# Graph attention on one core: the sort's digits in slots that ScalarE fills, one operation for the one-hots, a product and a sum for the picks

## The chip, the core and the metric

The kernel runs on one core of one Trainium2 chip. A core has TensorE (PE; its weight loads are PEld), VectorE (DVE), ScalarE (ACT), GpSimd (POOL) and SyncE (SP, which here only issues DMAs), each with its own instruction stream; they meet through semaphores. The metric is the device time of one execution in microseconds (us), the median of several.

## The reference

One layer of graph attention over 12500 nodes and 412500 edges, with a residual and a layer norm:

```python
qkv = x @ qkv_w + qkv_b                      # q, k: 4 heads x 8; v: 4 heads x 16
qe = q[s] * scale + (edge_attr @ q_rpe_w + q_rpe_b)
ke = k[t] + (edge_attr @ k_rpe_w + k_rpe_b)
ve = v[t] + (edge_attr @ v_rpe_w + v_rpe_b)
compat = einsum('ehd,ehd->eh', qe, ke)
attn = softmax of compat over the edges of each s
out = layernorm(x + segment_sum(ve * attn, s))
```

Here s is the node that gathers an edge's message and t the other end. The edges come sorted by t, but the softmax and the sum go by s.

## The kernel before

It has three stages. The tables stage counts the edges of each node s and computes keys, values and queries of all nodes. The sort stage writes, for every edge, a record of 100 floats to the place in DRAM that a counting sort by s gives it. The attend stage reads each node's records, in 98 blocks of 128 nodes, and computes softmax, sum and norm.

The change is in the sort. Its edges go in 808 units of 512 edges, each of four tiles of 128 (CT = 4). A node's number is split in two digits, the low 7 bits (128 values) and the rest (98 values); the arrays lo_f, hi_f and src_f hold both digits and the number for all edges. For a unit u:

- SyncE (load_loop, lines 526 to 539) loads attributes, numbers broadcast to all partitions (ids_b) and a window of the key and value table, into one of 8 slots. Before it reuses a slot it waits for the ranks and the features of unit u - 8. Each unit is a row of register steps, one table load and three DMA issues.
- VectorE makes one-hots of both digits (hots, lines 581 and 583); counts for each edge the earlier edges of its unit with the same number (ranks, line 592, four operations, each with a read of its accumulator); picks each edge's place from the table that TensorE looked up (picks, line 601, four custom operations, each with an accumulator read too); adds rank and place, and multiplies query and key (place, lines 612 and 613); sums the product over a head (total, line 617).
- TensorE adds the unit's counts to the table of free places (line 680, waits for hots and for the table copy), looks up the rows of the table (line 689) and computes the features (line 706).
- ScalarE makes the transposed one-hots (lines 724 to 733), copies the table from PSUM (line 742, waits for the counts of line 680; TensorE's next unit waits for it) and copies the records (line 717).
- GpSimd scatters the records, four indirect DMAs a unit (line 556), once place and total of the unit are done.

Each engine's order is written out by hand: 16 units at the head, then a loop whose body holds 8 units. VectorE's step u is: picks of u - 2, total of u - 3, ranks of u + 2, place of u - 2, one-hots of u + 2. ScalarE's step u: offsets of u + 2, table copy of u, turned of u + 2, records of u - 1.

## Time and profile before

| | us |
|---|---|
| median of 3 runs | 6195.86 (6191.55 to 6196.50) |
| the profiled execution | 6252.36 |
| its span, first to last instruction | 6250.6 |

The granted TensorE clock was 0.723 of full speed over the span. The profile comes from one execution, so durations and waits are read from it and set against its own 6252.36. A page of the profile gives each engine's busy time, and its groups of instructions with busy time, mean duration, and the engine's idle time just before them with what ended it ("issue": nothing that the profile shows; "remote": a semaphore whose last update it can't name). A timeline gives single instructions with their start and duration. The durations of consecutive instructions on one engine overlap a little, so what one costs its engine is read from start to start.

### The profile page before, as it was taken

Reading aid. Unit: us, or ns where it says so; the run is one execution under the profiler, and the core shown is the slowest. Engines: PE = TensorE matmul, PEld = TensorE weight load, DVE = VectorE, ACT = ScalarE, POOL = GpSimd, SP = SyncE. Lnnn points to the kernel's source line nnn. Section 1 sums busy time; section 2 is a strip of 40 time slices with the busy share of each in tenths; the row PEclk is TensorE's granted clock in tenths of the full one; section 3 lists DMA queues with packets and bytes.
Section 4 is the critical chain, followed back from the end, with each engine's and each line's share of the span. In section 5 each row is a group of like instructions: output and inputs, shape, how many; then the busy total and the mean of one; then the engine's idle time right before and its main releaser. Section 6 shows DMA issues by size and latency. Waiting matters only on the chain. (4 is left out here: it accounts for less than half of the span.)

```text
span 6250.6 us, 108230 instructions
## 1 busy us (share of the span) xinstructions
PE 3639.5 (58%) x22344; PEld 3313.1 (53%) x22344; DVE 4739.5 (76%) x18269; ACT 3094.1 (50%) x7584; POOL 3604.8 (58%) x4044
## 2 busy tenths in 40 slices
PE   5656555555555555555555655556555655486886
PEld 4545555555555455555555554545555555365665
DVE  9987777777777777777777777777777777698998
ACT  6965555555455555555555554545555545232332
POOL 0025666666666666666666666666666666564664
PEclk9986666666666766666666666676666666798999
DMA  3023333333333333333333333333333333697997
GB/s 81 19 63 113 111 108 111 108 109 107 112 110 108 111 108 111 108 111 109 108 111 108 111 111 106 111 108 111 108 111 108 111 108 112 233 363 278 365 363 264
DMA packets 423280, 848.16 MB, mean 136 GB/s; under 512 B 190271, under 2 KB 254072, under 8 KB 410362
## 3 DMA queue, kind: packets, MB, share of 16 engines
q1 hardware_dynamic: 305412, 399.40, 23.0%
q0 software_dynamic: 117824, 448.32, 19.5%
q14 instruction: 33, 0.27, 0.0%
q8 instruction: 11, 0.18, 0.0%
HBM read 671.35 MB, written 176.01 MB: 136 GB/s over the span
## 5 line engine op out<-in xcount | busy, mean ns | idle before, releaser
L556 POOL DMA_INDIRECT rec_dram<-recs,place_i x3232 | 3097.1, 958 | 1873.9 <-issue 1807.9
L592 DVE SCALAR_TENSOR_TENSOR matches<-ids_b,src_f,ps_const 128x128 bf16<-128x128 int16 (+3 forms) x3232 | 1646.0, 542 | 601.5 <-issue 559.7
L680 PE MATMUL ps_cnt<-hi_hot,lo_hot 128*128 128x98 bf16 x3232 | 383.2, 264 | 2113.3 <-DVE hi_hot L583 1071.6
L680 PEld LDWEIGHTS ps_cnt<-hi_hot,lo_hot 128*128 128x128 bf16 x3232 | 236.1, 123 | 2292.6 <-DVE hi_hot L583 1177.7
L689 PE MATMUL ps_look<-free_rec,lo_hotT 128*128 128x98 f32 x6464 | 1406.6, 388 | 1.2 <-ACT lo_hotT L730 1.2
L742 ACT ACTIVATE free_rec<-ps_cnt 128x98 f32<-128x98 f32 x808 | 198.8, 246 | 2412.7 <-remote 2244.6
L706 PE MATMUL ps_feat<-w_in,edge_in 115*128 115x128 f32 x6464 | 1325.8, 371 | 45.6 <-issue 44.0
L689 PEld LDWEIGHTS ps_look<-free_rec,lo_hotT 128*128 128x128 f32 x6464 | 1286.7, 295 | 1.5 <-ACT lo_hotT L730 1.5
L706 PEld LDWEIGHTS ps_feat<-w_in,edge_in 115*128 115x128 f32 x6464 | 1224.6, 281 | 52.4 <-issue 51.1
L1013 PE MATMUL ps_sum<-msg,ident 128*128 128x256 f32 x2744 | 624.3, 386 | 243.5 <-DVE msg L1227 243.5
L601 DVE CUSTOM_DVE_ANT_0 picked<-hi_hot,ps_look 128x98 f32<-128x98 bf16 x3232 | 643.7, 248 | 94.3 <-issue 90.0
L1013 PEld LDWEIGHTS ps_sum<-msg,ident 128*128 128x128 f32 x2744 | 518.9, 192 | 348.8 <-DVE msg L1227 281.4
L724 ACT ACTIVATE lo_hotT<-ids_b,minus_p 128x512 f32<-128x512 int16 x808 | 578.2, 716 | 5.7 <-DMA w_in<-kv_dram 5.7
L726 ACT ACTIVATE edge_in<-ids_b,minus_p 96x512 f32<-96x512 int16 x808 | 578.2, 716 | 0.0
L730 ACT ACTIVATE lo_hotT<-lo_hotT,one 128x512 f32<-128x512 f32 x808 | 576.9, 714 | 0.0
L733 ACT ACTIVATE edge_in<-edge_in,one 96x512 f32<-96x512 f32 x808 | 575.3, 712 | 0.0
L581 DVE TENSOR_TENSOR lo_hot<-lo_f,ps_const 128x512 bf16<-128x512 bf16 (+1 forms) x808 | 547.5, 678 | 19.9 <-issue 19.9
L592 DVE DVE_READ_ACCUMULATOR matches<-ids_b,src_f,ps_const 128x1 f32 x3232 | 261.4, 81 | 326.8 <-issue 309.7
L717 ACT ACTIVATE recs<-ps_feat 128x512 f32<-128x512 f32 x808 | 468.7, 580 | 22.7 <-remote 15.9
L583 DVE TENSOR_TENSOR hi_hot<-hi_f,ps_const 128x392 bf16<-128x392 bf16 (+1 forms) x808 | 446.1, 552 | 1.9 <-issue 1.6
L1172 ACT ACTIVATE ps_prob<-ps_lg,neg 128x56 f32<-128x56 f32 x392 | 109.2, 279 | 537.4 <-DVE neg L1062 537.4
L601 DVE DVE_READ_ACCUMULATOR2_ANT first<- 128x1 f32 x3232 | 256.1, 79 | 150.3 <-issue 147.3
(154 smaller groups left out, 3424.7 us busy)
## 6 DMA issues: line engine op xcount, KB each, us to landing
ids_b<-id_dram SPq DMA_DIRECT2D x808, 384.0 KB
rec_dram<-recs,place_i POOLq DMA_INDIRECT x3232
edge_in<-in_attr SPq DMA_DIRECT2D x808, 36.0 KB
w_in<-kv_dram SPq DMA_DIRECT2D x808, 36.0 KB
kv_dram<-y SPq DMA_DIRECT2D x14, 336.0 KB, 2.8
xt<-in_xT SPq DMA_DIRECT2D x14, 224.0 KB, 3.3
out_y<-y SPq DMA_DIRECT2D x6, 448.0 KB
src_i<-in_src_tiles SPq DMA_DIRECT2D x1, 1616.0 KB, 8.5
```

What stands on the lines that cost most here:

```text
L556: pool.indirect_dma_start(rec_dram[:, :], bass.IndirectOffsetOnAxis(place_i[j][:, m:m + 1], 0), recs[j][:, m, 0:REC], None).then_inc(scatt ...
L581: dve.tensor_tensor(lo_hot[j][:, :, :], lo_f[:, tiles].unsqueeze(2).broadcast_to((P, CT, P)), ps_const[:, 0:1, :].broadcast_to((P, CT, P)) ...
L592: last = dve.scalar_tensor_tensor(matches[j % NS][:, junk:junk + before], ids_b[j][:, 1, 0:before], src_f[:, bass.ds(u * CT + m, 1)], ps_c ...
L601: ins = dve.tensor_tensor_reduce(out=picked[j % NS][:, m, :], in0=hi_hot[j][:, m, :], in1=ps_look[j % NS][:, m, 0:NB], scale=1.0, scalar=0 ...
L680: last = nc.tensor.matmul(ps_cnt[:, 0:NB], lo_hot[j][:, m, :], hi_hot[j][:, m, :], start=False, stop=False, skip_group_check=True)
L689: last = nc.tensor.matmul(ps_look[j % NS][:, m, 0:NB], lo_hotT[j % NS][:, P * m:P * (m + 1)], free_rec[j % 2][:, :], start=True, stop=True)
L706: last = nc.tensor.matmul(ps_feat[j % 2][:, m, :], edge_in[j][0:K_ROWS, tile], w_in[j][0:K_ROWS, :], start=True, stop=True)
L724: act.activation(lo_hotT[j % NS][:, :], ids_b[j][:, 0, :], ACT.Abs, bias=minus_p[:, 0:1]).then_inc(lo_off, 1)
L726: act.activation(edge_in[j][0:WIN, :], ids_b[j][0:WIN, 2, :], ACT.Abs, bias=minus_p[0:WIN, 0:1]).then_inc(dst_off, 1)
L730: act.activation(lo_hotT[j % NS][:, :], lo_hotT[j % NS][:, :], ACT.Relu, scale=-1.0, bias=one[:, 0:1]).then_inc(lo_hotT_made, 1)
L733: act.activation(edge_in[j][0:WIN, :], edge_in[j][0:WIN, :], ACT.Relu, scale=-1.0, bias=one[0:WIN, 0:1]).then_inc(dst_hotT_made, 1)
L1013: last = nc.tensor.matmul(ps_sum[i][:, 0:SUM, :], ident[:, :], msg[i][:, k:k + SUM, :], start=(k == 0), stop=(k + SUM == S0))
```

## The change

The three arrays become one, dig_f, with the three numbers of an edge side by side. In the sort ScalarE copies the twelve numbers of a unit, five units ahead, into one of eight small slots (dig); VectorE reads them from there, at fixed addresses, as the scalars of the ranks and as the source of the one-hots. These are made by one operation for both digits (hot), with 128 columns for each digit. The four fused picks become one product over the unit (picks) and one sum (firsts). VectorE's step is put in another order: picks of u - 2, place of u - 3, one-hots of u + 2, ranks of u + 2, firsts of u - 2, total of u - 3. TensorE reads its one-hots from hot; its order, GpSimd's and SyncE's stay. The head is written out to match.

```diff
-        T["lo_f"] = digits.enter_context(nc.sbuf_tensor("lo_f", [P, NT], F32))
-        T["hi_f"] = digits.enter_context(nc.sbuf_tensor("hi_f", [P, NT], F32))
-        T["src_f"] = digits.enter_context(nc.sbuf_tensor("src_f", [P, NT], F32))
+        T["dig_f"] = digits.enter_context(nc.sbuf_tensor("dig_f", [P, NT, 3], F32))
...
-            dve.tensor_copy(src_f[:, :], src_i[:, :]).then_inc(narrowed, 1)
+            dve.tensor_copy(dig_f[:, :, 2], src_i[:, :]).then_inc(narrowed, 1)
...
-            act.activation(lo_f[:, :], lo_w[:, :], ACT.Copy).then_inc(widened, 1)
-            act.activation(hi_f[:, :], hi_w[:, :], ACT.Copy).then_inc(widened, 1)
+            act.activation(dig_f[:, :, 0], lo_w[:, :], ACT.Copy).then_inc(widened, 1)
+            act.activation(dig_f[:, :, 1], hi_w[:, :], ACT.Copy).then_inc(widened, 1)
...
-        lo_hot = [sb(f"lo_hot{c}", [P, CT, P], BF16) for c in range(NU)]
-        hi_hot = [sb(f"hi_hot{c}", [P, CT, NB], BF16) for c in range(NU)]
+        dig = [sb(f"dig{c}", [P, CT, 3]) for c in range(NU)]
+        hot = [sb(f"hot{c}", [P, CT, 2, P], BF16) for c in range(NU)]
...
             def hots(u, j):
-                tiles = bass.ds(u * CT, CT)
-                dve.tensor_tensor(lo_hot[j][:, :, :], lo_f[:, tiles].unsqueeze(2).broadcast_to((P, CT, P)),
-                                  ps_const[:, 0:1, :].broadcast_to((P, CT, P)), ALU.is_equal)
-                dve.tensor_tensor(hi_hot[j][:, :, :], hi_f[:, tiles].unsqueeze(2).broadcast_to((P, CT, NB)),
-                                  ps_const[:, 0:1, 0:NB].broadcast_to((P, CT, NB)), ALU.is_equal).then_inc(hots_made, 1)
+                dve.wait_ge(dig_made, u + 1)
+                dve.tensor_tensor(hot[j][:, :, :, :], dig[j][:, :, 0:2].unsqueeze(3).broadcast_to((P, CT, 2, P)),
+                                  ps_const[:, 0:1, :].unsqueeze(1).broadcast_to((P, CT, 2, P)), ALU.is_equal).then_inc(hots_made, 1)
...
-                        matches[j % NS][:, junk:junk + before], ids_b[j][:, 1, 0:before], src_f[:, bass.ds(u * CT + m, 1)],
+                        matches[j % NS][:, junk:junk + before], ids_b[j][:, 1, 0:before], dig[j][:, m, 2:3],
...
-            def pick(u, j, m):
-                if m == 0:
-                    dve.wait_ge(looked, u + 1)
-                ins = dve.tensor_tensor_reduce(
-                    out=picked[j % NS][:, m, :], in0=hi_hot[j][:, m, :], in1=ps_look[j % NS][:, m, 0:NB], scale=1.0, scalar=0.0,
-                    op0=ALU.mult, op1=ALU.add, accum_out=first[j][:, m:m + 1])
-                if m == CT - 1:
-                    ins.then_inc(placed, 1)
+            def picks(u, j):
+                dve.wait_ge(looked, u + 1)
+                dve.tensor_tensor(picked[j % NS][:, :, :], hot[j][:, :, 1, 0:NB], ps_look[j % NS][:, :, 0:NB], ALU.mult).then_inc(picked_all, 1)
+
+            def firsts(u, j):
+                dve.wait_ge(picked_all, u + 1)
+                dve.tensor_reduce(first[j][:, :], picked[j % NS][:, :, :], AX.X, ALU.add).then_inc(placed, 1)
...
                 if not ends(u, -2):
                     picks(u - 2, at(2))
-                total(u - 3, at(3))
+                place(u - 3, at(3))
                 if not ends(u, 2):
+                    prepare(u + 2, at(-2))
                     ranks(u + 2, *slot(j, turn, -2))
                 if not ends(u, -2):
-                    place(u - 2, at(2))
-                if not ends(u, 2):
-                    prepare(u + 2, at(-2))
+                    firsts(u - 2, at(2))
+                total(u - 3, at(3))
...
         def scalar_loop(act, general):
+            SOON = 5
...
+                if not ends(u, SOON):
+                    digits(u + SOON, slot(j, turn, -SOON)[0])
+
+            def digits(u, j):
+
+                if not starts(u, NU):
+                    act.wait_ge(ranked, u - NU + 1)
+                act.activation(dig[j][:, :, :], dig_f[:, bass.ds(u * CT, CT), :], ACT.Copy).then_inc(dig_made, 1)
+
+            for u in range(SOON):
+                digits(u, u)
```

How the order of instructions differs, in the loop's body. VectorE before, the end of a step's ranks and what follows up to the one-hots (the four picks and the total stand ahead of it; an ISA row between ranks sets an address; a rank's accumulator read is part of its row):

```order
L592 ISA
L592 SCALAR_TENSOR_TENSOR matches3,rank3<-ids_b3,src_f,ps_const 128x256
L592 ISA
L592 SCALAR_TENSOR_TENSOR matches3,rank3<-ids_b3,src_f,ps_const 128x384
L592 ISA
L592 SCALAR_TENSOR_TENSOR matches3,rank3<-ids_b3,src_f,ps_const 128x512
L612 TENSOR_TENSOR place_i7<-first7,rank7 128x4 [waits ranked,placed,kv_copied]
L613 TENSOR_TENSOR qk3<-recs7 128x128
L581 REGISTER_ALU
L581 TENSOR_TENSOR lo_hot3<-lo_f,ps_const 128x512
L583 REGISTER_ALU
L583 TENSOR_TENSOR hi_hot3<-hi_f,ps_const 128x392
```

And the picks before, at the start of VectorE's next step:

```order
L600 REGISTER_ALU
L601 ISA picked0,first0<-hi_hot0,ps_look0 128x98 [waits looked]
L601 ISA first0 128x1
L601 ISA picked0,first0<-hi_hot0,ps_look0 128x98
L601 ISA first0 128x1
L601 ISA picked0,first0<-hi_hot0,ps_look0 128x98
L601 ISA first0 128x1
L601 ISA picked0,first0<-hi_hot0,ps_look0 128x98
L601 ISA first0 128x1
```

VectorE now, one whole step (picked, place_i, hot, matches, first, recs are what picks, place, one-hots, ranks, firsts and total write):

```order
L598 TENSOR_TENSOR picked3<-hot7,ps_look3 128x392 [waits looked]
L609 TENSOR_TENSOR place_i6<-first6,rank6 128x4 [waits ranked,placed,kv_copied]
L610 TENSOR_TENSOR qk2<-recs6 128x128
L580 REGISTER_ALU
L581 TENSOR_TENSOR hot3<-dig3,ps_const 128x1024 [waits dig_made]
L590 SCALAR_TENSOR_TENSOR matches3,rank3<-ids_b3,dig3,ps_const 128x128 [waits loaded3,ranked]
L590 SCALAR_TENSOR_TENSOR matches3,rank3<-ids_b3,dig3,ps_const 128x256
L590 SCALAR_TENSOR_TENSOR matches3,rank3<-ids_b3,dig3,ps_const 128x384
L590 SCALAR_TENSOR_TENSOR matches3,rank3<-ids_b3,dig3,ps_const 128x512
L602 TENSOR_REDUCE first7<-picked3 128x4 [waits picked_all]
L614 TENSOR_REDUCE recs6<-qk2 128x4x4 [waits dotted]
```

The picks' eight rows became one here and one near the end, the address rows between the ranks are gone, and the one-hots stand ahead of the ranks. ScalarE before, one step (lo_hotT and edge_in are the transposed one-hots, free_rec the table copy, recs the records):

```order
L724 ACTIVATE lo_hotT0<-ids_b4,minus_p 128x512 [waits looked,loaded4]
L726 ACTIVATE edge_in4<-ids_b4,minus_p 96x512
L742 ACTIVATE free_rec1<-ps_cnt 128x98 [waits counted]
L729 REGISTER_ALU
L730 ACTIVATE lo_hotT0<-lo_hotT0,one 128x512 [waits lo_off]
L733 ACTIVATE edge_in4<-edge_in4,one 96x512 [waits dst_off]
L717 ACTIVATE recs1<-ps_feat1 128x4x128 [waits scattered1,feats]
```

ScalarE now, the same step:

```order
L725 ACTIVATE lo_hotT0<-ids_b4,minus_p 128x512 [waits looked,loaded4]
L727 ACTIVATE edge_in4<-ids_b4,minus_p 96x512
L743 ACTIVATE free_rec1<-ps_cnt 128x98 [waits counted]
L731 ACTIVATE lo_hotT0<-lo_hotT0,one 128x512 [waits lo_off]
L734 ACTIVATE edge_in4<-edge_in4,one 96x512 [waits dst_off]
L718 ACTIVATE recs1<-ps_feat1 128x4x128 [waits scattered1,feats]
L760 ISA [waits ranked]
L760 ACTIVATE dig7<-dig_f 128x12
```

Two rows are added at the end of the step, the copy of the digits and the setting of its address, and one register step (line 729) is gone; the operations ahead of them stand as before.

## Rows read from the trace of the kernel before

**Rows 1.** The page: busy time of the engines, then VectorE's costliest groups (section 5).

```profile
PE 3639.5 (58%) x22344; PEld 3313.1 (53%) x22344; DVE 4739.5 (76%) x18269; ACT 3094.1 (50%) x7584; POOL 3604.8 (58%) x4044
...
L592 DVE SCALAR_TENSOR_TENSOR matches<-ids_b,src_f,ps_const 128x128 bf16<-128x128 int16 (+3 forms) x3232 | 1646.0, 542 | 601.5 <-issue 559.7
L601 DVE CUSTOM_DVE_ANT_0 picked<-hi_hot,ps_look 128x98 f32<-128x98 bf16 x3232 | 643.7, 248 | 94.3 <-issue 90.0
```

**Rows 2.** Busy time in one stretch of 500 us inside the sort.

```profile
core 0: us, PE busy (x) PEld busy (x) DVE busy (x) ACT busy (x) POOL busy (x), PEclk, DMA share, GB/s
3000.00:3500.00 500.00, 281.74 (x1626) 262.70 (x1627) 359.89 (x1716) 256.11 (x491) 312.77 (x327) 0.67 0.36 110
```

**Rows 3.** Line 556, GpSimd's scatters: first and last start, idle time before them.

```profile
L556 POOL DMA_INDIRECT rec_dram<-recs,place_i x3232: 952/958/1216, 413.3 to 5376.6; - x191
...
  issue: 1807.9, 3154
```

**Rows 4.** Who waited for whom, 1000 to 5000 us (us in total, times, longest).

```profile
ACT free_rec L742 <- remote: 1845.4, 306, 12.1
DVE matches L592 <- issue: 715.8, 1184, 2.0
...
SPq L532 <- remote: 322.5, 161, 7.2
```

**Rows 5.** Timeline of VectorE: start us, us, engine line op out<-in.

```profile
3028.88 0.15 DVE L612 TENSOR_TENSOR place_i<-first,rank 128x4 int32<-128x4 f32 x1
...
3029.15 0.67 DVE L581 TENSOR_TENSOR lo_hot<-lo_f,ps_const 128x512 bf16<-128x512 bf16 x1
3029.75 0.54 DVE L583 TENSOR_TENSOR hi_hot<-hi_f,ps_const 128x392 bf16<-128x392 bf16 x1
3030.22 0.24 DVE L601 CUSTOM_DVE_ANT_0 picked<-hi_hot,ps_look 128x98 f32<-128x98 bf16 x1
...
3030.93 0.27 DVE L617 TENSOR_REDUCE recs<-qk 128x16 f32<-128x128 f32 x1
3031.13 0.33 DVE L592 SCALAR_TENSOR_TENSOR matches<-ids_b,src_f,ps_const 128x128 bf16<-128x128 int16 x1
...
3033.00 0.15 DVE L612 TENSOR_TENSOR place_i<-first,rank 128x4 int32<-128x4 f32 x1
```

**Rows 6.** The same, a few us later; in brackets the idle time before.

```profile
3038.16 0.35 DVE L592 SCALAR_TENSOR_TENSOR matches<-ids_b,src_f,ps_const 128x128 bf16<-128x128 int16 x1 [0.44 <-issue]
3038.88 0.08 DVE L592 DVE_READ_ACCUMULATOR matches<-ids_b,src_f,ps_const 128x1 f32 x1 [0.38 <-issue]
3040.96 0.48 DVE L592 SCALAR_TENSOR_TENSOR matches<-ids_b,src_f,ps_const 128x256 bf16<-128x256 int16 x1 [1.99 <-issue]
```

**Rows 7.** Timeline of GpSimd: a run of eight scatters and the next one.

```profile
3012.51 0.96 POOL L556 DMA_INDIRECT rec_dram<-recs,place_i  x1 [2.39 <-issue]
...
3021.34 0.96 POOL L556 DMA_INDIRECT rec_dram<-recs,place_i  x1 [0.30 <-issue]
3024.78 0.96 POOL L556 DMA_INDIRECT rec_dram<-recs,place_i  x1 [2.48 <-issue]
```

**Rows 8.** Timeline of SyncE's queue: two DMAs of three units.

```profile
3015.26 0.03 SPq L534 DMA_DIRECT2D edge_in<-in_attr  x1
...
3021.82 0.73 SPq L539 DMA_DIRECT2D w_in<-kv_dram  x1
3024.30 0.31 SPq L534 DMA_DIRECT2D edge_in<-in_attr  x1
...
3026.80 0.32 SPq L534 DMA_DIRECT2D edge_in<-in_attr  x1
```

**Rows 9.** Timeline of ScalarE in the same stretch.

```profile
3017.44 0.71 ACT L726 ACTIVATE edge_in<-ids_b,minus_p 96x512 f32<-96x512 int16 x1
3024.17 0.25 ACT L742 ACTIVATE free_rec<-ps_cnt 128x98 f32<-128x98 f32 x1 [6.02 <-remote]
```

**Rows 10.** Timeline of TensorE in the same stretch.

```profile
3018.30 0.51 PE L680 MATMUL ps_cnt<-hi_hot,lo_hot 128*128 128x98 bf16 x4 [0.29 <-DVE hi_hot L583]
```

More of the change, by code:

```diff
@@ L102, in tables_stage @@
     iota_row, iota_f, iota_p, ident, later = (T[k] for k in ("iota_row", "iota_f", "iota_p", "ident", "later"))
-    lo_f, hi_f, src_f, q_tab = (T[k] for k in ("lo_f", "hi_f", "src_f", "q_tab"))
+    dig_f, q_tab = T["dig_f"], T["q_tab"]
     base, deg, w_attr = (T[k] for k in ("base", "deg", "w_attr"))
@@ L399, in higher @@
                     last = act.activation(s_hi[i][:, k, :], ps_half[:, 0:NB + 1], ACT.Sign, scale=-1.0,
-                                          bias=hi_f[:, bass.ds(GT * g + GT - SIGNS + k, 1)])
+                                          bias=dig_f[:, bass.ds(GT * g + GT - SIGNS + k, 1), 1])
                 last.then_inc(hi_signs, 1)
@@ L437, in sort_stage @@
     iota_p, ident, later = (T[k] for k in ("iota_p", "ident", "later"))
-    lo_f, hi_f, src_f, base, w_attr, win_row, flag = (T[k] for k in ("lo_f", "hi_f", "src_f", "base", "w_attr", "win_row", "flag"))
+    dig_f, base, w_attr, win_row, flag = (T[k] for k in ("dig_f", "base", "w_attr", "win_row", "flag"))
     deg, y, more = (T[k] for k in ("deg", "y", "more"))
@@ L491, in sort_stage @@
         lo_off, dst_off = sem("lo_off"), sem("dst_off")
+        dig_made, picked_all = sem("dig_made"), sem("picked_all")
         kv_got = [sem(f"kv_got{c}") for c in range(NU)]
@@ L618, in total @@
                                   AX.X, ALU.add).then_inc(totalled, 1)
-            def picks(u, j):
-                for m in range(CT):
-                    pick(u, j, m)
             def prepare(u, j):
@@ L632, in step, with ahead @@
                     picks(u - 2, at(2))
-                total(u - 3, at(3))
+                place(u - 3, at(3))
                 if not ends(u, 2):
+                    prepare(u + 2, at(-2))
                     ranks(u + 2, *slot(j, turn, -2))
                 if not ends(u, -2):
-                    place(u - 2, at(2))
-                if not ends(u, 2):
-                    prepare(u + 2, at(-2))
+                    firsts(u - 2, at(2))
+                total(u - 3, at(3))
             def head():
+                at = lambda u: u % NU
+                def ahead(*units):
+                    for v in units:
+                        prepare(v, at(v))
+                        ranks(v, at(v), v // NU)
                 prepare(0, 0)
@@ L645, in head @@
                 prepare(1, 1)
-                at = lambda u: u % NU
                 for u in range(HEAD - 4):
                     picks(u, at(u))
+                    firsts(u, at(u))
                     place(u, at(u))
@@ L655, in head @@
                 ranks(u + 1, at(u + 1), (u + 1) // NU)
+                firsts(u, at(u))
+                ahead(u + 2)
                 place(u, at(u))
-                for v in (u + 2, u + 3):
-                    ranks(v, at(v), v // NU)
-                    prepare(v, at(v))
+                ahead(u + 3)
                 total(u, at(u))
                 picks(u + 1, at(u + 1))
-                for v in (u + 4, u + 5):
-                    ranks(v, at(v), v // NU)
-                    prepare(v, at(v))
-                place(u + 1, at(u + 1))
+                ahead(u + 4)
+                firsts(u + 1, at(u + 1))
+                ahead(u + 5)
             if general:
@@ L679, in step @@
                 for m in range(CT):
-                    last = nc.tensor.matmul(ps_cnt[:, 0:NB], lo_hot[j][:, m, :], hi_hot[j][:, m, :], start=False, stop=False,
+                    last = nc.tensor.matmul(ps_cnt[:, 0:NB], hot[j][:, m, 0, :], hot[j][:, m, 1, 0:NB], start=False, stop=False,
                                             skip_group_check=True)
```

## The prediction

> **What bounds the kernel now.** The page comes first: VectorE is the busiest engine at 76%, yet idle a quarter of the time, and its largest groups are line 592 (ranks) and line 601 (picks) [rows 1]. The stretch table says the same of the sort alone: 360 of 500 us for VectorE, 313 for GpSimd, 282 for TensorE, 256 for ScalarE [rows 2]. GpSimd's scatters run from 413.3 to 5376.6 us, 4963 us of the 6250.6; its 3232 scatters, four a unit, make 808 units of 6.14 us [rows 3]. All of the change that counts is in this stage.
>
> Next, what ends VectorE's idle time. Its largest group is "issue": 716 us in 1184 pieces before line 592, inside 4000 us, released by nothing that the profile shows [rows 4]. The timeline shows it in two ways. In one, a unit takes 3033.00 - 3028.88 = 4.12 us and no instruction waits [rows 5]. In the other, consecutive instructions without any wait between them start about 0.7 us apart, or a multiple of it (3038.16, 3038.88, 3040.96), while they run for 0.08 to 0.48 us [rows 6]. So 6.14 - 4.12 = 2.02 us a unit, 1630 us in all, is time in which VectorE has work and is not handed it.
>
> This is not VectorE's alone. GpSimd scatters two units in one run: first start 3012.51, last 3021.34, next run 3024.78 [rows 7]. Inside it SyncE, whose steps for a unit are all sequencer work, needs 3024.30 - 3015.26 = 9.04 us for a unit; just after it, 3026.80 - 3024.30 = 2.50 [rows 8]. ScalarE is held in the same stretch: TensorE has the counts of a unit at 3018.30 + 0.51 = 3018.81, and the copy that waits for them starts at 3024.17, when SyncE is quick again [rows 9, 10]. This late wake-up is most of ScalarE's 1845 us on "remote" [rows 4]. I call such stretches held, and the others free: a held stretch goes with a run of scatters, beginning and ending near 1.9 us after it (an estimate from the ends 3022.30 and 3024.17). A scatter takes 0.96 + 0.30 = 1.26 us [rows 7], a unit 5.05, so about 4.9 us of each 6.14 are held.
>
> **The change part by part.** VectorE's work without stalls, by start to start [rows 5]:
> - Removed: one-hots 0.60 + 0.47, picks 3030.93 - 3030.22 = 0.71; together 1.78.
> - Added, none of it in the trace. One-hots of 1024 columns: 120 more columns (512 against 392) cost 0.13 us, 1.08 ns each, so 0.60 + 512 x 1.08 ns = 1.15. The one operation makes 128 columns of the high digit where 98 were made, so fusing saves a start and pays 120 columns. The product of 392 columns from the same kinds of memory: 0.47, as line 583. The sum over 392: line 617 sums 128 in 3031.13 - 3030.93 = 0.20, plus 264 x 1.08 ns, 0.48. Together 2.10. Bounds for product and sum together: 0.71 (as the picks) and 1.2 (both as the 512-column operation). I take 0.95, since the column counts match.
> - Net: +0.32 us a unit, between +0.08 and +0.57. Were VectorE simply busy, 808 x 0.32 = 259 us slower.
>
> VectorE's instructions: before 21 on the engine a unit (8 for picks, 8 for ranks with their accumulator reads, 2 one-hots, 2 place, 1 total) and 6 address steps, of which four stand at the ranks; after 14 and one. 27 become 15, with a wait or two more (picked_all, dig_made). Stalls come by the instruction, 0.7 us each, and 2.02 us are about three a unit. Twelve fewer more than cover three, if what VectorE is handed is limited by number. I take its own stalls to go: it then needs 4.12 + 0.32 = 4.44 us a unit, and is 1.7 us early. The new own wait picked_all has place, one-hots and four ranks between producer and waiter (3 us of work), so it is met on arrival. dig_made is filled five units ahead. The one-hots now stand ahead of the ranks, so TensorE gets them earlier in a step by the ranks' 3033.00 - 3031.13 = 1.87 us [rows 5].
>
> ScalarE: one more copy of 12 columns (at most the 0.25 us of line 742 [rows 9]), one address step and a wait for ranks of three units back, long done. Busy 256.11/500 x 6.14 = 3.14 becomes 3.4 a unit: under 4.44, so nothing, unless it is on the path, then up to 0.25. ScalarE is late now because counts come after it asks for them; with one-hots early they come before. TensorE's program is the same, 3.5 us a unit [rows 2].
>
> Outside the loop: the three widenings write every third word; they are a few us in all and I add nothing.
>
> **What is late next.** Two things stand under 6.14.
> - GpSimd: 5.05 us of scatters plus its gap between runs, 2.48 [rows 7]. With runs of m units a unit takes 5.05 + 2.48/m: 6.29 at two, 5.88 at three, 5.67 at four. VectorE early means more finished units when GpSimd looks, so longer runs.
> - SyncE: its program is unchanged, and in a held stretch it needs 9.04 us for a unit. With 4.9 held us a unit it does 4.9/9.04 = 0.54 of its work there, and the other 0.46 costs 1.15 free us: 6.05 us a unit. Longer runs leave fewer free us, so loads fall behind, VectorE and ScalarE wait for them, GpSimd runs dry, and a free stretch comes. It waits for a free slot 322 us in 652 units, 0.5 a unit [rows 4], so the lower bound is 5.64; upper bound 6.05. Since the waits are themselves late wake-ups I stay near the upper: 5.98.
>
> Sum: 808 x (6.14 - 5.98) = 129 us off the profiled 6252.4 (span 6250.6 and 1.8 around it): 6123. The timed runs' median is 56.5 us under the profiled one, so 6067.
>
> A rule speaks against this. No row names what slows the sequencers. The Trainium skill ("Runtime: NRT & Kernel Launch", Instruction fetch mechanics) holds that instruction fetch is hidden, because dispatch is slower than the fills, save at a taken branch. By that rule fewer instructions relieve nothing and the sum would be +259 us. The trace disagrees in part: the 0.7 us steps of rows 6 lie far from a loop's branch.
>
> **The rivals.**
> - Much faster. SyncE's slack is real (5.64) and runs reach four units (5.67): 808 x 0.47 = 380 us off, 5816. For it: SyncE's waits; VectorE's large reserve. Against: its 9.04 us. 19%.
> - No change. GpSimd asks for a unit's total as soon as the previous one is queued, and in a held stretch hears of it only at its end; total stays last in the step, so runs stay at two units and 6.14 stands: 6196. 11%.
> - Slower, by VectorE. The stalls are a share of time and not of instructions (for it: they stop at once when the run ends), so 2.02 us stay and the longer operations are paid in full: 6196 + 259 = 6455; at half, 6325. It decides if less than 0.32 us a unit of stall goes. 18%.
> - Slower, by ScalarE: the extra copy delays the table copy that TensorE waits for, and its wait in a held stretch costs another late wake-up: 808 x 0.25 = 200 us, 6396. Against: ScalarE is idle half the time. 6%.
>
> **How the numbers follow.** Forecast 46%, by itself 5990 to 6150: 6067. The whole range reaches to the half-way points of the outer rivals and leaves about two in ten out: 5800 to 6290. A change under 0.2% (12 us) can't be told from none. Faster: 45 of the forecast's 46, the 19, and 3 of no change, 67%; the same: 9%; slower: 24%.
>
> **What would show it.** Idle on "issue" before VectorE's ranks falls from 716 us to under 200; its one-hots take near 1.2 us, product 0.55, sum 0.55; ScalarE's "remote" before the table copy shrinks; runs of scatters of three or more units appear; and new idle time stands at the waits for loads (VectorE's ranks or ScalarE's line 725, released by a DMA), with SyncE no longer waiting. The forecast is wrong if VectorE still stalls in 0.7 us steps, if runs stay at eight scatters, or if a unit falls below 5.8 us with SyncE still waiting.

## The result, and the profile after

| | before | after |
|---|---|---|
| median, us | 6196.18 (6191.55 to 6199.01, 4 runs) | 6412.99 (6404.22 to 6440.81, 4 runs) |
| profiled execution, its span | 6252.36, 6250.6 | 6414.70, 6413.0 |
| granted TensorE clock | 0.723 | 0.727 |

The ratio is 1.0355, 95% interval [1.0339, 1.0371]: 217 us slower, where 129 us faster was forecast, and above the forecast's range of 5800 to 6290. A later comparison gave 1.0366 [1.0349, 1.0384]. The profiled execution of the kernel before was itself 56 us above its median, so the two profiles show 162 of the 217 us.

The page of the kernel after, busy time and VectorE's groups of the change (against [rows 1]; busy us, mean ns of one, idle before it):

```profile
PE 3405.3 (53%) x22344; PEld 3084.7 (48%) x22344; DVE 4787.4 (75%) x12613; ACT 3172.6 (49%) x8392; POOL 3606.2 (56%) x4044
...
L590 DVE SCALAR_TENSOR_TENSOR matches<-ids_b,dig,ps_const 128x128 bf16<-128x128 int16 (+3 forms) x3232 | 1572.8, 541 | 3.6 <-issue 3.6
...
L598 DVE TENSOR_TENSOR picked<-hot,ps_look 128x392 f32<-128x392 bf16 x808 | 448.4, 555 | 1339.3 <-remote 1194.6
...
L581 DVE TENSOR_TENSOR hot<-dig,ps_const 128x1024 bf16<-128x1024 f32 x808 | 979.8, 1213 | 0.9 <-issue 0.9
...
L602 DVE TENSOR_REDUCE first<-picked 128x4 f32<-128x392 f32 x808 | 448.0, 554 | 11.6 <-issue 10.8
```

What was forecast of VectorE came: 12613 instructions for 18269; the idle time before the ranks fell from 601.5 us (559.7 of it on issue) to 3.6; one-hots take 1.21 us, product and sum 0.55 each. But 1339 us of idle time now stand before the product. GpSimd's scatters after (against [rows 3]: first and last start, idle time before them):

```profile
L556 POOL DMA_INDIRECT rec_dram<-recs,place_i x3232: 952/958/1216, 415.6 to 5539.1; - x191
...
  issue: 1488.6, 3143
  DVE place_i L609: 509.0, 73
```

They take 5123.5 us, 160 more than before, of 162 more in the span: 6.34 us a unit for 6.14. Nearly all of it is idle time of GpSimd, of which 509.0 us now stand in 73 waits, 7 us each, for VectorE's place. Who waited for whom, 1000 to 5000 us (against [rows 4]):

```profile
ACT free_rec L743 <- remote: 1766.4, 254, 17.9
...
PE ps_cnt L679 <- ACT free_rec L743: 1060.7, 179, 16.4
DVE picked L598 <- remote: 930.0, 163, 11.9
...
POOL rec_dram L556 <- DVE place_i L609: 370.9, 52, 9.1
PE ps_feat L705 <- issue: 356.5, 357, 2.6
```

From the starts of all scatters follows how long the runs are. A run ends here where GpSimd idles for more than 1.5 us, its gap is that idle time, and a cycle goes from its first scatter to the next run's first. Each cell has the number of cycles, their mean length, the mean gap, and the cycle's length for each unit (four scatters) in it, in us. Runs of other lengths, most of them cut inside a unit by a pause of 1.66 us, are left out (35 before, 28 after).

| scatters in the run | before: cycles, mean, gap, a unit | after |
|---|---|---|
| 4 | 42, 6.70, 1.95, 6.70 | 32, 8.98, 4.24, 8.98 |
| 8 | 306, 12.19, 2.38, 6.10 | 7, 14.48, 4.22, 7.24 |
| 12 | 30, 18.22, 2.71, 6.07 | 142, 17.89, 3.01, 5.96 |
| 16 | none | 57, 26.09, 5.34, 6.52 |
| 20 | none | 9, 34.23, 7.61, 6.85 |

Runs did get longer, as forecast, but their gaps grew with them, and single units came between. Runs of three units are no dearer than the runs of two were before (5.96 us a unit against 6.10); the loss stands in runs of four and five units and in single ones. Where the line at 1.5 us is put moves the counts (at 1.3 us, 172 runs of twelve and 35 of sixteen) and not this picture. The timeline after shows what happens inside a run, in four pieces: VectorE, ScalarE, TensorE, and GpSimd's run of twelve (start, us, instruction, idle before it).

```profile
3033.47 0.28 DVE L614 TENSOR_REDUCE recs<-qk 128x16 f32<-128x128 f32 x1
3041.96 0.56 DVE L598 TENSOR_TENSOR picked<-hot,ps_look 128x392 f32<-128x392 bf16 x1 [8.22 <-remote]
```

```profile
3033.20 0.71 ACT L727 ACTIVATE edge_in<-ids_b,minus_p 96x512 f32<-96x512 int16 x1
3042.11 0.25 ACT L743 ACTIVATE free_rec<-ps_cnt 128x98 f32<-128x98 f32 x1 [8.20 <-remote]
```

```profile
3027.58 1.10 PE L688 MATMUL ps_look<-free_rec,lo_hotT 128*128 128x98 f32 x8
...
3031.03 0.33 PE L679 MATMUL ps_cnt<-hot 128*128 128x98 bf16 x4 [1.33 <-issue]
...
3034.89 0.36 PE L705 MATMUL ps_feat<-w_in,edge_in 115*128 115x128 f32 x1 [1.17 <-issue]
3037.01 0.27 PE L705 MATMUL ps_feat<-w_in,edge_in 115*128 115x128 f32 x1 [1.77 <-issue]
3039.11 0.37 PE L705 MATMUL ps_feat<-w_in,edge_in 115*128 115x128 f32 x1 [1.83 <-issue]
3042.51 0.49 PE L679 MATMUL ps_cnt<-hot 128*128 128x98 bf16 x4 [3.03 <-ACT free_rec L743]
```

```profile
3024.88 0.96 POOL L556 DMA_INDIRECT rec_dram<-recs,place_i  x1 [2.72 <-issue]
...
3038.95 0.96 POOL L556 DMA_INDIRECT rec_dram<-recs,place_i  x1 [0.30 <-issue]
```

Counting products, lookups, copies and counts from the first unit on tells which belong together: the product at 3041.96 needs the lookup that ended at 3027.58 + 1.10 = 3028.68, and the copy at 3042.11 the counts that ended at 3031.03 + 0.33 = 3031.36. Both engines came to their wait at 3033.7 and 3033.9, long after its condition was met, and went on 2.0 and 2.2 us after the run's end at 3039.91. TensorE meanwhile started one matmul every 2.1 us without any wait, and SyncE made a step about every 0.7 us (from its table load at 3031.98 to the first DMA issue of its next unit at 3038.38 it needs 6.4 us; right after the run, from 3042.08 to 3042.74, 0.7). So this is not a late wake-up from an unmet wait: inside a long run VectorE and ScalarE stand still, TensorE and SyncE crawl, and GpSimd alone keeps its pace. The label "remote" stands for it. Counted so over units 60 to 739, all 186 pauses over 1.5 us before the product and all 278 before the table copy had their condition met before the engine arrived. In the kernel before that was so in 80 of ScalarE's 315; in the other 235 the condition was met while it stood, and it stood on for 5.5 us (median).

### The profile page after: what moved, and what is told of

It reads as the page before. It is cut to its first block and busy times, and to the rows that moved or that the text cites. A ratio compares the mean times of both kernels' runs of the same rounds, so it can differ in the third digit from the quotient of the medians.

```text
span 6413.0 us, 99854 instructions
## 1 busy us (share of the span) xinstructions
PE 3405.3 (53%) x22344; PEld 3084.7 (48%) x22344; DVE 4787.4 (75%) x12613; ACT 3172.6 (49%) x8392; POOL 3606.2 (56%) x4044
## 5 line engine op out<-in xcount | busy, mean ns | idle before, releaser
L590 DVE SCALAR_TENSOR_TENSOR matches<-ids_b,dig,ps_const 128x128 bf16<-128x128 int16 (+3 forms) x3232 | 1572.8, 541 | 3.6 <-issue 3.6
L598 DVE TENSOR_TENSOR picked<-hot,ps_look 128x392 f32<-128x392 bf16 x808 | 448.4, 555 | 1339.3 <-remote 1194.6
L679 PE MATMUL ps_cnt<-hot 128*128 128x98 bf16 x3232 | 351.9, 248 | 2064.3 <-ACT free_rec L743 1266.1
L679 PEld LDWEIGHTS ps_cnt<-hot 128*128 128x128 bf16 x3232 | 252.9, 119 | 2210.2 <-issue 2076.4
L688 PE MATMUL ps_look<-free_rec,lo_hotT 128*128 128x98 f32 x6464 | 1268.3, 360 | 3.6 <-DVE first L602 2.8
L688 PEld LDWEIGHTS ps_look<-free_rec,lo_hotT 128*128 128x128 f32 x6464 | 1154.0, 268 | 4.4 <-ACT lo_hotT L731 3.2
L581 DVE TENSOR_TENSOR hot<-dig,ps_const 128x1024 bf16<-128x1024 f32 x808 | 979.8, 1213 | 0.9 <-issue 0.9
L602 DVE TENSOR_REDUCE first<-picked 128x4 f32<-128x392 f32 x808 | 448.0, 554 | 11.6 <-issue 10.8
L398 ACT ACTIVATE s_hi<-ps_half,dig_f 128x99 bf16<-128x99 f32 x1212 | 303.6, 366 | 56.8 <-PE ps_sign L358 56.6
L1238 DVE TENSOR_TENSOR msg<-rec,ps_prob 128x1280 f32<-128x1280 f32 x196 | 287.9, 1469 | 2.0 <-ACT prob_s L1194 1.4
```

What stands on the lines that cost most here:

```text
L581: dve.tensor_tensor(hot[j][:, :, :, :], dig[j][:, :, 0:2].unsqueeze(3).broadcast_to((P, CT, 2, P)), ps_const[:, 0:1, :].unsqueeze(1).broad ...
L590: last = dve.scalar_tensor_tensor(matches[j % NS][:, junk:junk + before], ids_b[j][:, 1, 0:before], dig[j][:, m, 2:3], ps_const[:, CT - m: ...
L679: last = nc.tensor.matmul(ps_cnt[:, 0:NB], hot[j][:, m, 0, :], hot[j][:, m, 1, 0:NB], start=False, stop=False, skip_group_check=True)
L688: last = nc.tensor.matmul(ps_look[j % NS][:, m, 0:NB], lo_hotT[j % NS][:, P * m:P * (m + 1)], free_rec[j % 2][:, :], start=True, stop=True)
```

## The experiments

One thing first, since every number below depends on it. I call the executions that were timed together on one chip a session. The kernel before itself took (medians) either 5391 to 5400 us or 6196 to 6273 us in a session; all its executions in one session agreed within 0.3%, and one chip showed both levels in different sessions. I call these free and held sessions. In a free one SyncE's register steps follow each other at 0.16 us (mean from start to start; 0.35 in the held profile of the kernel before) through scatters 0.3 us apart, and GpSimd alone is the bound: 5.06 us a unit. Comparisons are within a session.

**Four edits of one kind each.** The first is the changed kernel with the order of before (`picks(u-2); total(u-3); ranks(u+2); firsts(u-2); place(u-2); prepare(u+2)`).

> The changed kernel's operations and slots, with the order of steps of the kernel before: picks of u - 2, total of u - 3, ranks of u + 2, firsts and place of u - 2, one-hots of u + 2. Theory A (VectorE, no longer stalled, arrives early at the wait for TensorE's lookups, is woken late in a held stretch, and GpSimd's scatters then gather in longer runs with longer gaps): the cause is that VectorE is ahead, whatever the order, so the time stays near the changed kernel's 6413, within 60 us. Theory B (the new order is the cause: place and total of a unit come a step later, behind the wait for the lookup): the time falls below 6200. Theory C (the longer operations are simply paid): 6413 within 20 us, and VectorE's idle time before picks stays.

The second is the kernel before, with `dig[j][:, :, 0:1]`, `dig[j][:, :, 1:2]` and `dig[j][:, m, 2:3]` for lo_f, hi_f and src_f, and ScalarE's copies.

> The kernel before with only the digit slots: ScalarE copies twelve numbers a unit, VectorE's ranks and its two one-hot operations read them from fixed addresses; the fused picks and the order stay. VectorE has 21 instructions a unit and one address step instead of six. Theory A (stalls go by the number of VectorE's instructions and steps; being ahead is what hurts): part of the 716 us of issue stalls before the ranks goes, VectorE waits for lookups in their place, and the time is between the two kernels, 6200 to 6350. Theory C (longer operations): no operation is longer, so it is not slower than 6196, and faster by up to 100 us. Theory D (ScalarE's copy): 6350 to 6413.

The third has the copies, and nobody reads them: `dig_f[:, tiles, 0:1]` for lo_f, and so on.

> The kernel before with ScalarE's copy of the digits alone: nobody reads the slots, VectorE reads the long array as before (every third word of it). Prices ScalarE's extra instruction, address step and wait. Theory D (ScalarE's copy is what costs: it delays the table copy): 6350 or more. Theories A, B and C: within 40 us of 6196.

The fourth is the changed kernel with VectorE's steps shifted:

```diff
-                    picks(u - 2, at(2))
-                place(u - 3, at(3))
+                    picks(u - 3, at(3))
+                place(u - 4, at(4))
...
-                    firsts(u - 2, at(2))
-                total(u - 3, at(3))
+                    firsts(u - 3, at(3))
+                total(u - 4, at(4))
```

> The changed kernel with picks and firsts of u - 3 and place and total of u - 4 in VectorE's step u, one unit later than now: TensorE has one more unit of time for the lookup that VectorE asks for. Theory A: VectorE's idle time before line 598 (1339 us in the changed kernel) falls by half or more; if that wait is what costs, the time falls to 6250 or below; if the late wake-ups then only move to ScalarE and TensorE, whose chain of count, table copy and next count is the same, it stays within 50 us of 6413. Theory C (longer operations): no change, 6413 within 30 us.

Measured, in a free session: 5403.5, 5401.7, 5403.3 and 5408.7 us beside 5399.6, ratios 1.0008, 1.0004, 1.0006 and 1.0017, intervals about ±0.001. The first two once more (5394.7 and 5393.6 beside 5391.3) and the first a third time (5396.9 beside 5394.1) were free too. They decide nothing of the 217 us; they show that without holding the parts of the change cost 0.2% at most, though VectorE works 4826.6 us in the first. The waits of its third run, 1000 to 4500 us:

```profile
ACT recs L716 <- DMA rec_dram<-recs,place_i: 1238.9, 525, 7.7
PE ps_feat L703 <- ACT recs L716: 1112.4, 502, 7.6
...
POOL rec_dram L556 <- issue: 810.8, 2660, 0.3
```

ScalarE and TensorE wait for scatters, and GpSimd never idles over 0.3 us. The line that headed [rows 4], ScalarE's wait before the table copy, does not appear.

**The changed kernel again.**

> The changed kernel itself, with the kernel before on the same chip. In the runs so far on this chip the kernel before takes 5400 us and not 6196: its traces show no held stretch and GpSimd's scatters follow each other at 0.3 us. If held stretches are what the change costs time by, it is within 10 us of the kernel before wherever these are missing, and about 217 us slower where the kernel before takes 6196. If the longer operations or the order cost by themselves, it is slower on both.

A held session: 6430.6 beside 6197.4, ratio 1.0366. The loss is real where sequencers are held. The changed kernel as it stands was never timed in a free one.

**Versions side by side in one execution.** Since nothing here chooses whether a session is held, I put several versions into one kernel: VectorE's loop over the units is cut into parts, each with its own step, as in `for k in range(3): part(dve, old_order(k + 1), PARTS[k], PARTS[k + 1])`. The pace of a part is (last start - first start)/(scatters - 1) x 4. Each of these kernels with parts was executed once, beside the kernel before.

> Four versions of the sort in one execution, one after the other, each over about 192 units, so that they are compared on one chip: (1) VectorE's operations and order of before, numbers from the long array, no copies by ScalarE (units 16 to 207), (2) the same with the digit slots filled by ScalarE and read by VectorE (208 to 399), (3) the changed kernel's operations in the old order (400 to 599), (4) the changed kernel's operations in its own order (600 to 791). The pace is read from GpSimd's scatters; in the kernel before it was between 6.08 and 6.14 us a unit in all of these stretches, in the changed one between 6.30 and 6.37. Theory A (being ahead, whatever the order): part 2 between 6.1 and 6.3, part 3 near 6.3, part 4 near 6.33. Theory B (the order): parts 1 to 3 at 6.14 or less, part 4 at 6.33. Theory C (longer operations simply paid): part 2 at 6.1, parts 3 and 4 at 6.33. Theory D (ScalarE's copies): parts 2 to 4 at 6.33. On a chip where the kernel before takes 5400 all parts run at GpSimd's 5.06.

A held session (6319.7, before 6197.0). Its scatters, a row for each part:

```profile
L564 POOL DMA_INDIRECT rec_dram<-recs,place_i x768: 952/958/1039, 522.1 to 1688.0; - x192
```
```profile
L564 POOL DMA_INDIRECT rec_dram<-recs,place_i x768: 952/958/1068, 1689.2 to 2849.9; - x192
```
```profile
L564 POOL DMA_INDIRECT rec_dram<-recs,place_i x800: 952/958/1042, 2856.2 to 4118.1; - x160
```
```profile
L564 POOL DMA_INDIRECT rec_dram<-recs,place_i x768: 952/958/1082, 4121.3 to 5342.4; - x192
```

6.08, 6.05, 6.32 and 6.37 us. Neither the order (0.05 between the last two) nor the slots and copies (-0.03) are the cause: it lies in the operations. How small a difference counts depends on the picks. In the kernel before, with fused picks, the pace over 80 units stays between 6.11 and 6.15; in the second profile of the changed kernel it goes from 6.24 to 6.52, and over 152 units, the length of the parts below, from 6.32 to 6.44 (6.27 to 6.43 in the first). So with product and sum differences under some 0.2 aren't told from none, with fused picks those under 0.05.

**Which operation, and whether its work or its number counts.** Part 3 adds `dve.tensor_tensor(spare[:, 0:2, :], ...)` over 256 columns, part 4 four operations of 4 columns, all between ranks and place, read by nobody.

> Again several versions in one execution, in the old order of steps and all with the digit slots, to tell which operation costs the 0.31 us a unit that lay between the second and the third part of the run before (6.02 and 6.33). (1) slots alone, units 32 to 183; (2) with the one operation for both one-hots, 184 to 335 (one instruction less, its work 0.08 us longer); (3) slots and one more VectorE operation of 256 columns, some 0.3 us, whose result nobody reads, 336 to 487; (4) slots and four more VectorE operations of 4 columns each instead, 488 to 639; (5) slots with picks as product and sum, 640 to 799 (six instructions less with the accumulator reads, 0.24 us longer). Theory C (VectorE's work is simply paid, microsecond by microsecond): (1) 6.02, (2) 6.1, (3) 6.33, (4) 6.2 to 6.4, (5) 6.27. Theory A (fewer instructions let VectorE run ahead into unmet waits, and longer runs of scatters come of it): (2) 6.02 to 6.1, (3) at most 6.1, (4) at most 6.1, since both slow VectorE down and hide nothing, (5) 6.25 or more. Theory E (instructions are what is rationed in held stretches): (4) is clearly above (3). Where the kernel before takes 5400 all parts run at 5.06.

A held session (6303.0, before 6249.3). First the part with slots alone, then those with four small operations, and with product and sum:

```profile
L565 POOL DMA_INDIRECT rec_dram<-recs,place_i x608: 956/962/1038, 620.1 to 1549.3; - x152
```
```profile
L565 POOL DMA_INDIRECT rec_dram<-recs,place_i x609: 956/962/1246, 3414.2 to 4369.2; - x153
```
```profile
L565 POOL DMA_INDIRECT rec_dram<-recs,place_i x637: 955/962/1069, 4369.2 to 5375.8; - x160
```

Runs are counted with the same 1.5 us, away from a part's edges:

| part | us a unit | runs of 8, of 12 or more |
|---|---|---|
| slots, fused picks | 6.12 | 44, 16 |
| and one operation for the one-hots | 6.13 | 44, 15 |
| and one more operation of 256 columns | 6.15 | 52, 8 |
| and four more of 4 columns | 6.28 | 71, 1 |
| product and sum for the picks | 6.33 | 0, 46 |

The one large operation takes 0.42 us, and the next instruction starts 0.33 us after it; it costs 0.02 us a unit, which isn't told from none. The four small ones keep the engine for 0.30 us, up to the start of the next, and cost 0.16. So beside fused picks VectorE's microseconds are not paid one by one (theory C falls), while four more instructions are paid for (theory E holds, on this one pair). The picks as product and sum cost 0.21 although they are six instructions fewer, and with them runs of two units are gone. Longer runs alone don't explain that yet: with fused picks and no small operations added, the runs of twelve took 6.05 to 6.12 us a unit in the parts of these two kernels, as the runs of eight did (6.03 to 6.11); beside product and sum, in the same old order, runs of twelve took 6.18 and 6.19.

**Around product and sum.** Part 2 puts `firsts(u - 2)` directly behind `picks(u - 2)`; parts 3 and 4 add work as above; part 5 does picks, sum and place of u - 3.

> Versions with picks as product and sum, in one execution, all with the digit slots, two one-hot operations and the old order; the part with these picks took 6.33 us a unit in the run before, the one with the fused picks 6.12. (1) as there, units 32 to 183; (2) the sum directly behind the product, as the fused picks do it, 184 to 335; (3) the sum late again, and four more operations of 4 columns each, which make the number of VectorE's instructions nearly that of the fused picks, 336 to 487; (4) instead one more operation of 256 columns, 0.3 us, 488 to 639; (5) picks, sum and place one unit later, 640 to 799. Theory A (with few instructions VectorE runs ahead into waits that are not yet met and wakes late from them): (1) 6.33, (2) 6.3, (3) 6.2 or less, (4) 6.25, (5) 6.2 or less. Theory E (every VectorE instruction is rationed in held stretches, and the late sum costs by itself): (2) 6.15, (3) 6.45, (4) 6.35, (5) 6.33. Where the kernel before takes 5400 all parts run at 5.06.

A held session (6489.6, before 6258.2): 6.34, 6.47, 6.48, 6.50 and 6.40 us. Product and sum cost as much in the first part of a kernel as in the last, so their place in it is not the cause. Theory A said that more instructions or a later lookup would heal it. Nothing did: that form of it, waits unmet on arrival, is wrong, as the timeline above shows too. The added work of parts 3 and 4 (0.14 and 0.17) isn't told from none here: part 2, without any, is 0.13 above part 1. One thing in part 3 does speak for run length. Its four small operations brought runs of two units back, some 30 of them beside 25 of three, and in this one part the runs of two took 6.18 us a unit and those of three 6.71.

**Runs kept short.** GpSimd waits, before some units, until the scatters of the unit before have landed:

```diff
                 if not starts(u, LAG):
+                    sent, sent_turn = slot(j, turn, LAG + 1)
+                    if most and (j - LAG) % most == 0:
+                        pool.wait_ge(scattered[sent], 16 * CT * sent_turn + 16 * CT)
```

> GpSimd is made to stop between scatters: before every second unit (or every unit, or every fourth) it waits until the scatters of the unit before have landed, so that a run can't be longer than that. All with the digit slots, two one-hot operations, the old order. (1) fused picks, no stop, units 32 to 139; (2) fused picks, stop every second unit, 144 to 283; (3) fused, every unit, 288 to 331; (4) picks as product and sum, every unit, 336 to 379; (5) the same, every second unit, 384 to 523; (6) every fourth unit, 528 to 651; (7) no stop, 656 to 799. Theory A in the form that is left (what costs is that runs of scatters get longer: three and four units instead of two, with gaps longer than in proportion): (1) 6.1, (2) 6.1 to 6.2, (5) 6.2 or less and so faster than (7) at 6.33, (6) like (7). If product and sum cost whatever the runs are: (5) is not below (7), and 0.2 or more above (2). Parts (3) and (4): about 5.05 us of scatters and a gap of 2.4 or more a unit, 7.4 or more, both alike. Where the kernel before takes 5400: (1) and (7) 5.06, the stops 1 to 2.4 us for each.

> The same kernel with stops once more, since the run before fell where the kernel before takes 5394 us and no sequencer is held; there the stops cost 2.1 us each. Parts: (1) fused picks, no stop, units 32 to 139; (2) fused, stop every second unit, 144 to 283; (3) fused, every unit, 288 to 331; (4) product and sum, every unit, 336 to 379; (5) every second unit, 384 to 523; (6) every fourth, 528 to 651; (7) no stop, 656 to 799. Where sequencers are held: if long runs of scatters are what product and sum cost by, (5) is 6.2 or less against 6.33 or more in (7), and (2) about (1) at 6.1. If product and sum cost whatever the runs are, (5) is 0.2 or more above (2), and not below (7).

The first fell in a free session (6048.4, before 5394.2): 5.06 without stops, 6.12 with a stop every second unit for either kind of picks, 7.62 and 7.61 with one every unit. The second was held (6462.7, before 6272.5). Its rows of product and sum, stopped every second unit, every fourth, and not at all:

```profile
L565 POOL DMA_INDIRECT rec_dram<-recs,place_i x560: 956/962/1081, 2937.6 to 3785.8; - x187
```
```profile
L565 POOL DMA_INDIRECT rec_dram<-recs,place_i x497: 955/962/1072, 3812.3 to 4599.7; - x166
```
```profile
L565 POOL DMA_INDIRECT rec_dram<-recs,place_i x572: 955/962/1074, 4623.7 to 5535.1; - x191
```

6.07, 6.35 and 6.38 us a unit; fused picks took 6.14 without stops and 6.10 with one every second unit, and both kinds 7.67 and 7.68 with one every unit. With runs of two units product and sum cost nothing, and an added wait makes the sort 0.3 us a unit faster. The stop every fourth unit (6.35) isn't told from no stop.

**The whole changed kernel with stops**, before units 0, 3 and 6 of each eight, or before every second.

> The changed kernel whole, with GpSimd waiting before units 0, 3 and 6 of each eight until the scatters of the unit before have landed, so that runs are of three, three and two units. Where sequencers are held: in the changed kernel the cycles of three units took 17.89 us, 5.96 a unit, and what made it 6.33 were the longer and the single ones. If long runs are the cost, this gives 5.9 to 6.0 a unit, 6020 to 6110 in all, faster than both kernels. If three units are already too long (gaps of 3.7 instead of 2.8 as with the old order): 6250 to 6400. Where they are not held (the kernel before at 5395): 3 stops of 2.1 us in eight units, 0.8 us a unit, about 6040.

> The changed kernel whole, stopped in the same way before every second unit. Where sequencers are held: 6.07 a unit as in the part with product and sum, about 6200, 210 us under the changed kernel and level with the kernel before; if the changed kernel's own order or one-hots cost beside the runs, 6300 or more. Where they are not held: 4 stops of 2.1 us in eight units, 1.05 us a unit, about 6240.

A held session, before 6251.4. Up to three units a run: 6498.8, ratio 1.0394 [1.0377, 1.0412]. Two: 6222.9, ratio 0.9956 [0.9939, 0.9973]. So the stops take the whole loss of the change away where sequencers are held, and leave it 0.4% under the kernel before. This kernel was not timed in a free session, where the same stops in the parts cost 1.06 us a unit. Its scatters, and its waits from 1000 to 5000 us:

```profile
L556 POOL DMA_INDIRECT rec_dram<-recs,place_i x3232: 956/962/1217, 415.2 to 5347.4; - x191
```
```profile
PEld ps_feat L708 <- issue: 1652.6, 387, 6.7
ACT recs L721 <- DMA rec_dram<-recs,place_i: 1400.5, 387, 6.0
```

Its 363 cycles of two units take 12.07 us with a gap of 2.23. The waits before the table copy and before the product are no longer among the nine largest, and ScalarE's largest is the one for scatters, as in a free session. With stops for three a run, 150 cycles of three units take 18.66 us (gap 3.72), 122 of two 12.87 (gap 2.93) and 53 single ones 8.57. My expectation of 6020 to 6110 for it was wrong: cutting the runs of four units off saves nothing (1.0394 times the kernel before, against 1.0355 and 1.0366 without stops), and next to runs of three even those of two are dearer, 6.44 us a unit against 6.03.

**The picks alone undone** in the whole changed kernel (the four fused picks at the step's start, no late sum), and the slots alone.

> The changed kernel whole with one part of it undone: the picks are the four fused operations of the kernel before, at the step's start, and the late sum is gone. Slots, ScalarE's copies, the one operation for the one-hots and the new order stay. Where sequencers are held: if the product and sum are what lets runs grow to three units, runs are of two units again, 6.0 to 6.1 a unit, and the time is that of the kernel before or up to 1% less; if the new order or the early one-hots do it too, runs of three stay and the time is 2% or more above it. Where they are not held: that of the kernel before within 0.2%.

> The kernel before whole with the digit slots alone, once more, for a chip where sequencers are held: in the run by parts this took 6.02 us a unit against 6.07 with the long array beside it. 808 x 0.05 = 40 us less than the kernel before, 0.65%, if that difference is real; within 0.2% if it was only the chance of where the parts lay. Where they are not held: 5394 to 5402 as before.

A free session: 5399.3 and 5394.2 beside 5393.1. The first once more: 5398.8 beside 5392.6, free again. They say nothing about held sessions. So it is not shown that undoing the picks alone heals the whole changed kernel; the parts show it only for the old order of steps.

## Why the prediction was wrong, point by point

- **VectorE's stalls go: right.** 601.5 us to 3.6, and all new durations within 0.1 us. That stalls come by the instruction and not by time fits the one pair that tests it, beside fused picks: four small operations cost 0.16 us a unit, one large 0.02. The Trainium skill ("Runtime: NRT & Kernel Launch", Instruction fetch mechanics) holds that instruction fetch is hidden except at a taken branch, and the trace agrees: in the profile of the kernel before the two queues that the profile labels "instruction" move 44 packets in all and none between 600 and 5200 us, where the held stretches are; in that of the kernel after none either. What I took from that rule, that fewer instructions relieve nothing, does not follow: the stalls stand where nothing is fetched, and they went. No run shows what holds the sequencers.
- **ScalarE's copy costs nothing: right** (ratio 1.0006 in a free session, not above 0 in the parts).
- **"Runs of m units: 5.05 + 2.48/m": the step that failed.** I took the gap between runs as constant. It is 3.01 us at three units, 5.34 at four, 7.61 at five and 4.24 after a single one, where the formula has 2.48. At the forecast's own run lengths a unit took 5.96 and 6.52 us instead of 5.88 and 5.67, and single units 8.98 instead of 7.53. Weighted by their number, the after column of the table makes 6.34. The trace before could have told me: its thirty runs of three units already took 6.07 us a unit, no less than the runs of two, and most of its runs (306) were of two units.
- **Why the gap grows is in part argued.** A held stretch is not only a stretch at another pace. In 290 of the 306 runs of eight before the change ScalarE stood before the table copy from 5.6 us (median) after the run's start to 1.9 us after its end, a pause of 6.0; in 29 of the 30 runs of twelve it stopped at the same point and the pause was 11.6. After the change it stopped later, at 8.9 us in runs of twelve (119 of 142) and 12.2 us in runs of sixteen (50 of 57), with pauses of 9.5 and 11.0 us. The chain of counts, table copy and lookup stands still in such a pause, so I take it that work is missing afterwards and GpSimd waits for it; no run changes the pause alone.
- **A slip in the same formula.** 5.05 us holds the 0.30 us after each scatter, and 2.48 stands in the place of the last of them, so 0.30 is counted twice. The run of [rows 7] took (3024.78 - 3012.51)/2 = 6.14 us a unit, and the formula says 6.29. Put right, 5.05 + 2.18/m gives 5.78 at three units and 5.60 at four, farther still from what was measured. The forecast of 5.98 went by SyncE and doesn't change by it.
- **"A new wait is met on arrival" and therefore free: half right.** The new wait, of the sum for its product, costs 11.6 us in all. But the old wait before the product was met on arrival too, in all 186 pauses counted, and 1339 us of idle time stand there all the same. It is the same with ScalarE: the early one-hots did bring the counts before it asks for them, in all 278 pauses, and its wait before the table copy fell only from 1845 to 1766 us.
- **SyncE bounds at 5.98: wrong.** VectorE's and ScalarE's idle time at load waits stayed under 4 us each, and SyncE still waited for free slots for 236 us from 1000 to 5000 us (322 before), where the forecast had it no longer waiting. So SyncE did not set the pace, and the 6.14 - 5.98 of the sum rests on a bound that never applied.
- **Two rivals have the time by luck.** "Slower, by VectorE" (6325 to 6455) holds the 6413 measured, and "slower, by ScalarE" (6396) is 17 us from it; both are wrong in their mechanism. The first needed stalls that stay; they went, and beside fused picks the one-hots, 0.08 us longer, cost 0.01 us a unit, which isn't told from none. The second needed a copy that costs, and in the parts it costs nothing.
- None of the rivals had that longer runs themselves cost. A row for it was there: in [rows 9] ScalarE stood from 3018.15 to 3024.17 with its counts ready at 3018.81, and I read it as a late wake-up of fixed kind instead of asking how it would be in a run half as long again.

What stays open: what holds the sequencers and why some sessions are free of it; why exactly product and sum, and not slots or one-hots in one operation, tip the runs from two units to three; and why three units at a time cost no more than two beside fused picks but do beside product and sum in the old order. Product and sum take the most instructions out (six), and VectorE then hands over three units in the time of two; that is argued, not shown.

## What to carry to other kernels

A stall that one engine shows may go together with another engine's short bursts. Before removing it, ask what happens to the burst and to everything that rests while it lasts. Don't extend a gap read at one burst length to another, and put a formula for the new case to the old one first: it has to give the time that the old trace shows. If executions fall into two groups, put the versions into parts of one execution, and check that the kernel before has the same pace in all of them. Where long bursts starve the rest, a wait that cuts them can pay: here two units a run gave 6222.9 us where the same kernel without stops took 6430.6 in another held session. That only regained the time of the kernel before, and where nothing is held a stop costs 2.1 us.

## What the runs showed of the hardware that was not expected

- The same kernel on one core takes 5391 or 6249 us on the same chip in different sessions. Against the profile of the kernel with slots alone, which is free, only the sort differs: 4106 us there and 4963 in the kernel before, and 872 and 874 us behind the last scatter's start. In held sessions SyncE and VectorE start instructions some 0.7 us apart while GpSimd issues indirect DMAs, and TensorE 2.1 us apart late in a run of twelve (3034.89, 3037.01, 3039.11). In free ones nothing of it is seen, through 576 scatters in a row 0.3 us apart.
- In a held run VectorE and ScalarE rest until about 2 us after the last scatter even where their wait is met (186 and 278 pauses, all of those counted). No instruction is fetched meanwhile (no packet of those queues from 600 to 5200 us).
- Beside fused picks, four VectorE operations of 4 columns cost 0.16 us a unit and one of 256 columns 0.02, though both keep the engine for about 0.3 us (one part each, in one execution).
